# Post-norm decoder layer on one core: the low-rank product in plain fp32, the first two norms' scaling on ScalarE, and one more stage between gate and expansion

## What is computed

```
x = layernorm(x + attention(x))            # 32 heads of 32, 8 kv heads, rope, causal softmax, wo
x = layernorm(x + conv3(x, ctx))           # 3 taps over features, each tap scaled by a cosine
                                           # similarity of neighbouring ctx columns
x = layernorm(x + 2 * ffn(x))              # ffn: low = x A^T  (8 experts x rank 16 = 128 columns)
                                           # logits = x Wr^T + br (8 columns)
                                           # out = (low * 8 softmax(logits)) B
```

## Time and profile before

| | before |
|---|---|
| median of 3 runs | 1571.94 us (1571.41 to 1572.42) |
| profiled execution | 1568.54 us |
| its span | 1566.8 us |
| mean granted TensorE clock | 0.981 |
| TensorE matmuls busy | 1402.8 us (90%) |
| VectorE busy | 1215.3 us (78%) |
| ScalarE busy | 859.7 us (55%) |
| GpSimd busy | 969.3 us (62%) |

### The profile page before, as it was taken

One profiled execution on the slowest core, in us unless ns is written; L12 is line 12 of the kernel. 1 busy time (PEld: TensorE's weight loads), 2 busy tenths in 40 slices (PEclk: granted clock), 3 DMA queues, 4 the chain that ended last, 5 costly groups with the idle time before them and its releaser, 6 DMA issues. The chain is left out here.

```text
span 1566.8 us, 32397 instructions
## 1 busy us (share of the span) xinstructions
PE 1402.8 (90%) x8288; PEld 1051.4 (67%) x8288; DVE 1215.3 (78%) x4094; ACT 859.7 (55%) x3196; POOL 969.3 (62%) x873
## 2 busy tenths in 40 slices
PE   6899898999999898999985899999999999999985
PEld 4566666666666666666662677777777777777774
DVE  5777677776777677776776588888888888888886
ACT  5777777777777777777775233333333333333332
POOL 3766666666666666666664566656666666666652
PEclk9999999999999999999997999999999999999996
DMA  6343434444443434344456765565555655556541
GB/s 223 106 135 108 131 113 132 113 132 121 123 134 108 132 112 132 115 135 120 121 171 181 188 147 148 156 156 134 145 141 147 161 139 143 145 141 155 147 108 41
DMA packets 109005, 213.03 MB, mean 136 GB/s; under 512 B 26656, under 2 KB 32288, under 8 KB 108960
## 3 DMA queue, kind: packets, MB, share of 16 engines
q1 hardware_dynamic: 108960, 212.51, 49.0%
HBM read 131.83 MB, written 34.47 MB: 106 GB/s over the span
## 5 line engine op out<-in xcount | busy, mean ns | idle before, releaser
L439 PE MATMUL wo_ps<-weights,halves 128*128 128x512 f32 x2304 | 572.2, 400 | 12.1 <-DVE weights L617 12.1
L701 ACT ACTIVATE pexp<-sm,smin 128x128 f32<-128x128 f32 x1024 | 398.5, 391 | 209.0 <-DVE smin L568 168.8
L439 PEld LDWEIGHTS wo_ps<-weights,halves 128*128 128x128 f32 x2304 | 422.7, 189 | 128.9 <-issue 34.6
L1050 PE MATMUL wo_ps<-weights,halves 128*128 128x512 f32 x1488 | 398.6, 401 | 2.0 <-DVE yz L1152 2.0
L1421 POOL TENSOR_TENSOR prods<-prod,prods 128x512 fp32r<-128x512 f32 x192 | 267.0, 1392 | 197.7 <-ACT prods L1333 196.7
L821 POOL TENSOR_TENSOR pn<-pexp,prec 128x512 f32<-128x512 f32 x256 | 267.3, 1044 | 180.4 <-DVE prec L575 180.4
L1050 PEld LDWEIGHTS wo_ps<-weights,halves 128*128 128x128 f32 x1488 | 273.5, 190 | 60.0 <-issue 3.7
L1333 ACT CAST prods<-prod 128x512 fp32r<-128x512 f32 x192 | 118.7, 619 | 326.8 <-DVE prod L1192 318.7
L568 DVE CUSTOM_DVE_ANT_0 sm<-s_ps,mask_t 128x128 f32<-128x128 f32 x1024 | 237.4, 288 | 14.7 <-PE s_ps L469 5.1
L1061 PE MATMUL conv_ps<-prods,weights 128*128 128x512 f32 x576 | 174.7, 412 | 41.2 <-POOL prods L1421 39.8
L575 DVE RECIPROCAL prec<-psum_row 128x4 f32<-128x4 f32 x256 | 44.8, 175 | 201.3 <-ACT pexp L701 201.1
(11 more groups left out here) (103 smaller groups left out, 1732.7 us busy)
## 6 DMA issues: line engine op xcount, KB each, us to landing
att<-sim_scratch SPq DMA_DIRECT2D x192, 252.0 KB
pt<-blocks SPq DMA_DIRECT2D x640, 64.0 KB, 2.0
ctx_t<-in_ctx SPq DMA_DIRECT2D x32, 576.0 KB, 4.7
raw<-in_xT SPq DMA_DIRECT2D x32, 512.0 KB, 3.6
raw<-ot_scratch SPq DMA_DIRECT2D x32, 512.0 KB, 6.5
xn<-in_x SPq DMA_DIRECT2D x32, 512.0 KB, 7.2
out<-late SPq DMA_DIRECT2D x32, 512.0 KB, 3.0
ot_scratch<-ot SPq DMA_DIRECT2D x63, 256.0 KB, 2.1
```

The source lines that it names most:

```text
L439: mm = pe.matmul(qkv_ps[(par + g) % 2][:], xs[:, par, xl, k], w_sb[:, wl, g, k], start=(k == 0 and n == 0), stop=(k == KT - 1 and n == 2))
L701: ins = nc.scalar.activation(pexp[:, c % 2, i * P:(i + 1) * P], sm[:, c % 2, i * P:(i + 1) * P], ACT.Exp, bias=smin[:, c % 2, i:i + 1], sc ...
L1050: mm = pe.matmul(wo_ps[n][:], os_t[:, par, ol, k], wo_sb[:, wl, k, n * BANK:(n + 1) * BANK], start=(k == 0 and m == 0), stop=(k == KT - 1 ...
```

## The change

In `part2`:

- `reduce_rank` multiplies the unsplit fp32 transpose `xt` by an unsplit fp32 `wa_t`: eight products of 136 columns instead of sixteen fp32r matmuls of 272. `low_x2` and the first two steps of `route` go, `gate_low` reads PSUM, and `wa_t` is loaded by one DMA (544 KB) at the start of part 2. The two pieces in part 1 that split `wa` go; `wx` stays.
- VectorE's `normalise` becomes `normalise1` and `normalise2` on ScalarE (activation with scale and shift). `average` makes the negated mean for all norms, `invert_root` the shift.
- `turn_low`, `high_lt` and `low_lt` of a sequence move from the end of its step f to the start of its step z, and slots and orders shift.

```
 # slots and TensorE
-    CONV_AT = (8, 10, 12, 14, 15, 17)
-    FIRST_CONV_AT = (11, 13, 15, 17, 18, 20)
+    CONV_AT = (9, 11, 13, 15, 17, 20)
+    FIRST_CONV_AT = (11, 13, 15, 17, 19, 20)
         def reduce_rank(t):
-            wait(pe, xt_lo, after(t, 2, 2))
+            wait(pe, xt_in, after(t, 2, 2))
             for k in range(KT):
-                for xl in range(2):
-                    mm = pe.matmul(ffn_place(t)[0][:, 0:2 * LOWW], xt[:, xl, k],
-                                   wa_sb[:, k].rearrange("p l n -> p (l n)"),
-                                   start=(k == 0 and xl == 0), stop=(k == KT - 1 and xl == 1))
+                mm = pe.matmul(ffn_place(t)[0][:, 0:LOWW], xt[:, k], wa_t[:, k * LOWW:(k + 1) * LOWW],
+                               start=(k == 0), stop=(k == KT - 1))
         # step
-                if valid(z) and s == 2:
-                    expand(z)
+                if valid(z):
+                    if s == 1:
+                        turn_low(z)
+                    if s == 3:
+                        expand(z)
                 if valid(f):
-                    if s in (9, 10):
-                        turn_x2(f, par, s - 9)
-                    if s == 13:
+                    if s in (11, 12):
+                        turn_x2(f, par, s - 11)
+                    if s == 14:
                         reduce_rank(f)
-                    if s == 15:
-                        turn_low(f)
 # SyncE
+        sp.dma_start(wa_t[:], wa).then_inc(consts_in, 16)
 # VectorE
             elif n == 1:
                 wait(dve, conv_done, after(t, UNITS, TAPS * (half + 1)))
+                wait(dve, normed[1], after(t - 1, 1, 1))
-            if n == 2:
-                dve.tensor_scalar(nmean3[:], mv[n][:, 0:1], -1.0, None, ALU.mult)
+            dve.tensor_scalar(nmean[n][:], mv[n][:, 0:1], -1.0, None, ALU.mult)
-        def normalise(t, par, n):
-            ...
-            dve.tensor_scalar(dst, src, mv[n][:, 0:1], rstd[n][:], ALU.subtract, ALU.mult).then_inc(normed[n], 1)
-        def low_x2(t, n):
-            ...
-            dve.tensor_tensor(dst[:, 1], ffn_place(t)[n][:], dst[:, 0].bitcast(F32), ALU.subtract).then_inc(xt_lo, 1)
-            dve.tensor_copy(lowhi[:], ffn_place(t)[0][:, LOWW:2 * LOWW]).then_inc(low_step, 1)
-            dve.tensor_tensor(low[:], ffn_place(t)[0][:, 0:LOWW], lowhi[:], ALU.add).then_inc(low_step, 1)
-            dve.tensor_tensor(logit[:], low[:, HR:LOWW], br_t[:], ALU.add).then_inc(low_step, 1)
+            dve.tensor_tensor(logit[:], ffn_place(t)[0][:, HR:LOWW], br_t[:], ALU.add).then_inc(low_step, 1)
         # order of a step now: add(c,0,1) count(c,0,1) average(c,0) | low_lt(z) add(z,2,0) add(z,2,1) |
         # multiply(c,0) | add(f,1,1) count(f,1,1) average(f,1) | multiply(c,1) | count(z,2,0)
         # count(z,2,1) average(z,2) | multiply(c,2) | add(t,0,0) count(t,0,0) | multiply(c,3)
         # multiply(c,4) add(c,1,0) count(c,1,0) | route(f) | multiply(c,5) | gate_low(f)
 # ScalarE
+        def normalise1(t, par):
+            wait(act, shifted[0], after(t, 1, 1))
+            nc.scalar.activation(x1[:, par, 1:D + 1], yz[:, 0], ACT.Identity, bias=shift[0][:],
+                                 scale=rstd[0][:]).then_inc(normed[0], 1)
+        def normalise2(t, par):
+            wait(act, shifted[1], after(t, 1, 1))
+            nc.scalar.activation(x2[:, par], yz[:, 1], ACT.Identity, bias=shift[1][:],
+                                 scale=rstd[1][:]).then_inc(normed[1], 1)
         # order of a step now: high_o(t+1) high_lt(z) normalise1(c) high_prod(c,0) high_prod(c,1)
         # normalise2(f) high_prod(c,2) normalise3(z) copy_x2(f,0) high_prod(c,3) copy_x2(f,1)
         # high_prod(c,4) gates(f) high_prod(c,5)
 # GpSimd
             pool.tensor_tensor(rstd[n][:], var[n][:], power[:], ALU.pow).then_inc(rstd_done[n], 1)
-            if n == 2:
-                pool.wait_ge(rstd_done[n], after(t, 1, 1))
-                pool.tensor_tensor(shift3[:], nmean3[:], rstd[n][:], ALU.mult).then_inc(shifted, 1)
+            pool.wait_ge(rstd_done[n], after(t, 1, 1))
+            pool.tensor_tensor(shift[n][:], nmean[n][:], rstd[n][:], ALU.mult).then_inc(shifted[n], 1)
         # order of a step now: invert_root(c,0) low_o(t+1,0) low_prod(c,0) invert_root(f,1)
         # low_prod(c,1) invert_root(z,2) low_prod(c,2) low_o(t+1,1) low_prod(c,3..5)
```

More of the change, by code:

```diff
@@ L100, in later_weights @@
 def later_weights(weights):
-    hi, lo = (weights[:, part * NG * KT * BANK:(part + 1) * NG * KT * BANK] for part in range(2))
+    lo = weights[:, NG * KT * BANK:2 * NG * KT * BANK]
     both = weights[:].rearrange("p (l m) -> p l m", l=2)
@@ L916, in part2 @@
     late = sb("late", [P, 2, 2, D])
-    xt = sb("xt", [P, 2, KT, S], F32R)
+    xt = sb("xt", [P, KT, S])
+    wa_t = sb("wa_t", [P, KT * LOWW])
     br_t = sb("br_t", [P, H])
     id_t = sb("id2_t", [P, P])
-    lowhi = sb("lowhi", [P, LOWW])
-    low = sb("low", [P, LOWW])
     logit = sb("logit", [P, H])
@@ L933, in part2 @@
     rstd = [sb(f"rstd{n}", [P, 1]) for n in range(3)]
-    nmean3 = sb("nmean3", [P, 1])
-    shift3 = sb("shift3", [P, 1])
+    nmean = [sb(f"nmean{n}", [P, 1]) for n in range(3)]
+    shift = [sb(f"shift{n}", [P, 1]) for n in range(3)]
     x2, res = late[:, 0], late[:, 1]
@@ L966, in part2 @@
     held = sem("held2")
-    shifted = sem("shifted")
+    shifted = [sem(f"shifted{n}") for n in range(3)]
     stored = [sem("stored0"), sem("stored1")]
@@ L1120, in _ @@
         steps(pe, step, 0, B - 1, LEAD, TAIL - 3)
+        convolve(B - 2, 4)
+        turn_low(B - 3)
         convolve(B - 2, 5)
@@ L1292, in _ @@
         average(B - 1, 0)
+        low_lt(B - 3)
         add(B - 2, 0, 1, 1)
-        normalise(B - 1, 1, 0)
+        count(B - 2, 1, 1)
+        average(B - 2, 1)
         for m in range(PB):
             multiply(B - 1, 1, m)
-        count(B - 2, 1, 1)
-        average(B - 2, 1)
-        multiply(B - 1, 1, 3)
-        normalise(B - 2, 0, 1)
-        multiply(B - 1, 1, 4)
         finish(B - 3)
-        low_x2(B - 2, 0)
-        multiply(B - 1, 1, 5)
-        low_x2(B - 2, 1)
+        for m in range(PB, UNITS):
+            multiply(B - 1, 1, m)
         add(B - 1, 1, 1, 0)
@@ L1351, in normalise3 @@
         def normalise3(t, par):
-            wait(act, shifted, after(t, 1, 1))
+            wait(act, shifted[2], after(t, 1, 1))
             wait(act, stored[par], arrivals(t, par) - 16)
-            nc.scalar.activation(res[:, par], y3[:], ACT.Identity, bias=shift3[:], scale=rstd[2][:]).then_inc(normed[2], 1)
+            nc.scalar.activation(res[:, par], y3[:], ACT.Identity, bias=shift[2][:], scale=rstd[2][:]).then_inc(normed[2], 1)
         def step(t, par):
@@ L1361, in step @@
                 high_o(t + 1, 1 - par)
+            if valid(z):
+                high_lt(z)
             if valid(c):
+                normalise1(c, 1 - par)
                 high_prod(c, 0)
@@ L1382, in step @@
                 high_prod(c, 5)
-            if valid(f):
-                high_lt(f)
         steps(act, step, 0, B - 1, LEAD, TAIL - 3)
+        high_lt(B - 3)
+        normalise1(B - 1, 1)
+        normalise2(B - 2, 0)
         for m in range(UNITS):
             high_prod(B - 1, m)
-            if m in (3, 4):
-                high_x2(B - 2, m - 3)
+            if m in (2, 3):
+                copy_x2(B - 2, m - 2)
         normalise3(B - 3, 1)
+        normalise2(B - 1, 1)
         gates(B - 2)
-        high_x2(B - 1, 0)
+        copy_x2(B - 1, 0)
         high_lt(B - 2)
-        high_x2(B - 1, 1)
+        copy_x2(B - 1, 1)
         gates(B - 1)
@@ L1427, in step @@
             c, f, z = t - 1, t - 2, t - 3
+            early = not at_step(t, 0) and not at_step(t, 1)
             if valid(c):
                 invert_root(c, 0)
-            early = not at_step(t, 0) and not at_step(t, 1)
             if valid(t + 1) and early:
@@ L1438, in step @@
                 low_prod(c, 1)
-            if valid(t + 1) and early:
-                low_o(t + 1, 1 - par, 1)
+            if valid(z):
+                invert_root(z, 2)
             if valid(c):
@@ L1445, in step @@
                 low_o(2, 0, 1)
-            if valid(z):
-                invert_root(z, 2)
+            if valid(t + 1) and early:
+                low_o(t + 1, 1 - par, 1)
             if valid(c):
```

113 lines of the change are left out of this document (40 added, 73 removed).

## The result

| | before | after |
|---|---|---|
| median, on one chip | 1572.02 us | 1511.24 us (1509.29 to 1512.58) |
| ratio of medians | | 0.9613 (0.9596 to 0.9629) |
| profiled execution | 1568.54 us | 1512.58 us |
| its span | 1566.8 us | 1510.7 us |

Forecast were 1525 us and a range of 1513 to 1549.

The account below looks back on a forecast made before the run. TensorE was taken as nearly the bound, held up by waits for GpSimd's products; 48.1 us gained in periods plus 0.8, less 2.5 for the load, made 46.4, forecasting 1525.5 us, range 1513 to 1549.

Parts of the forecast that it names:

- the period: Steady steps of part 2: from 21.31 to 19.65 us, 48.1 us gained over 29 periods.
- the drain: After the last step: between 2 us gained and 3 lost, taken as nothing.
- the start of part 2: First steps of part 2: 2.5 us lost to the wa_t load, 0.8 gained as half a step's worth.
- the step from one execution to the median: Whole kernel: median put 3.4 us above the profiled execution, 1522.1 to 1525.5 us.
- the bound: Steps of part 2: TensorE's own work, 19.6 us per sequence, becomes the bound alone as 1.7 us of waiting goes.
- the order laid out by hand: One step of part 2: each engine's times set against TensorE's; all its waits go, thin margins 0.2, 0.5, 0.8 us.
- rival A: Steps of part 2: thin margins fail because VectorE and GpSimd still take turns; period 20.35, 1545.8 us; chance 0.21.
- D: Step boundary in part 2: a ring of waits sets the old 21.31 us period again, 1572 us; chance 0.04.
- B: Low rank on TensorE: plain fp32 costs four passes, 4.0 us, slower at 1589.5 us; chance 0.06.
- C: Low rank on TensorE: faster passes make it 1.5 us, 16 us less, 1509 us; chance 0.03.
- the low rank: TensorE in each step: eight plain fp32 products, two passes each at 0.125 us, 2.0 us, no change.
- 0.05 added for restarts: Steady period of part 2: 0.05 us added for TensorE restarts at the thin margins, giving 19.65 us.

Follow-up runs that it names:

- e1: Changed kernel with the low-rank product computed twice into the same bank; 1566.16 us, ratio 0.9976.
- e10: Changed kernel with each plain fp32 low-rank product on 272 columns instead of 136; 1565.30 us, ratio 0.9957.
- e7: Kernel before with only the plain fp32 low rank (no low_x2, wa_t loaded at the start of part 2); 1562.41 us, ratio 0.9954.
- e3: Changed kernel with the low rank split again into fp32r matmuls, low_x2 back on VectorE; 1534.87 us, ratio 0.9785.
- e11: The changed kernel itself, run again on one chip beside e12 and e13; 1510.06 us, ratio 0.9614.
- e12: Changed kernel with the wa_t load put behind the first loads of part 2, run beside e11; 1511.07 us, ratio 0.9612.
- e4: Changed kernel with norms 1 and 2 scaled by VectorE again, without the two shifts; 1532.29 us, ratio 0.9771.
- e13: As e12, and VectorE scales the three norms left after the last step; 1507.93 us, ratio 0.9599.
- e2: Same kernel as e12 in another session: changed kernel with wa_t loaded after the first loads of part 2; 1508.78 us, ratio 0.9618.
- e5: Changed kernel with turn_low, high_lt and low_lt back at the end of step f; 1521.33 us, ratio 0.9695.
- e14: Kernel before with GpSimd's second low_o moved behind low_prod 2; 1563.31 us, ratio 0.9948.
- e8: Kernel before with only normalise1 and normalise2 moved to ScalarE; 1558.48 us, ratio 0.9926.
- e6: Changed kernel with e3's and e4's edits together, leaving only slots, orders and the longer pipeline; 1575.38 us, ratio 1.0036.
- e9: Changed kernel with the low-rank product on 72 of its 136 columns; 1509.36 us, ratio 0.9597.

## Why the prediction was right in kind and wrong in size

Forecast and measured time differ by 14.3 us, and no single step of the forecast carries that: 5.0 us are the period, 3.6 the drain, 3.1 the start of part 2 (1.4 gained where 1.7 were to be lost), 4.6 the step from one execution to the median; 2.0 went the other way, ahead of part 2. What would bound the steady step and which waits would go was forecast right.

**Right: the bound.** The steady step is TensorE's own work. The 19.6 us read from the last full step became 19.48, and e1 shows that each us added to TensorE is a us of time.

**Right: the order laid out by hand.** Against the trace of the step that begins at 1176.58 or 1196.06: `low_lt` ended at 2.4 (forecast 2.6), the first multiply came at 5.1 (5.1), product 0 was ready at 7.9 (7.8), `normalise2` ended at 10.5 (10.6), product 1 at 10.6 (10.5), product 2 at 13.2 (13.3), the transposes' copies at 14.9 (15.1), the gate at 19.0 (19.4). All of these are within 0.4 us, so rival A (a wait comes back) fell. Some of it is luck. x1 was ready at 4.4, not 4.9, and did not set the first multiply: VectorE was adding norm 3 until then. And the turns between VectorE and GpSimd that A was built on did stay; they cost these two engines time, but TensorE no wait. D (a ring) fell with e1. B fell by its price, not by its rule. A product is two records of two clocks a column (e10), so four clocks a column, where fp32r takes one: the work of four passes. But a clock for each of 136 columns is 0.057 us, and 32 of those are 1.8 us; B, and the forecast too, put 0.125 on a pass, which is what 272 columns cost. The forecast's two passes came out near the truth because each record takes two clocks a column. The time lies nearer to C's 1509 than to the forecast, but C's mechanism, a low rank of 1.5 us, is not what happened either.

**Wrong in size: the low rank.** I took 2.0 us because sixteen fp32r matmuls take that the earlier trace rows and called it no change, though the earlier trace rows gave 0.11 to 0.12 a pass. It is 1.85: the fp32r matmul of 272 columns costs 0.125 where its columns at 2.4 GHz, one clock each, make 0.113, and the plain fp32 record of 136 columns, two clocks each, costs 0.116. This is 0.15 us in each of 29 periods, 4.4 us. With 0.05 added for restarts that didn't come, and 0.03 more TensorE work elsewhere than I read, the period is 0.17 shorter than the forecast: 5.0 us.

**Wrong: the drain, 0 forecast, 3.6 measured.** The plain fp32 low rank is on the path there, twice, ahead of the gate. Before, two subtractions and two sums of VectorE stood around it, and they are gone. e7, which has only this edit, has a drain of 40.1 us from the last projection against 45.5, but at a mean granted clock of 0.82 against 0.73. The cleaner pair is e3 and the changed kernel, which differ in the low rank alone and have the same mean clock, 0.83: 43.9 us against 41.9. So about 2 us are the low rank (e11 and e12, with the same drain, differ by 1.3). The two ScalarE scalings work against it: with VectorE in their place the drain is 1.5 to 2.8 us shorter (e4, e13). I had seen both signs and let them cancel. The clock differs too. The drain of the kernel before and of the changed one, columns as in the earlier trace rows:

```profile
1521.30:1566.80 45.50, 24.70 (x90) 18.08 (x89) 29.67 (x63) 10.66 (x19) 13.35 (x16) 0.73 0.16 51
```
```profile
1468.80:1510.70 41.90, 22.54 (x94) 16.16 (x92) 23.07 (x55) 14.11 (x23) 13.99 (x19) 0.83 0.18 57
```

The mean granted clock is 0.73 and 0.83 of 2.4 GHz, a mixture of the two levels, and TensorE idles less in the second. The last low-rank product took 2.85 us before, at a mean clock of 0.66, and 2.1 after, at 0.88; at the full clock the two cost 2.01 and 1.85. How much of the 3.6 us is the clock stays open.

**Wrong: the start.** I charged 2.5 us for the load of `wa_t`, taking its transfer as time added one to one. It is about half of that: 1.3 us later came the first product after the start of part 2, and the runs above give 1.1 to 1.3 on average. And the rest of the first steps, priced at half a step's gain, 0.8, gained 2.7 us. That the first matmul of part 2 came 2.0 us later is scatter: in runs whose first parts are alike (after, e1, e2, e4, e11, e12) it begins between 856.1 and 860.0.

**The bridge to the median.** I carried the 3.4 us between the profiled execution before and its median over to the kernel after, where the profiled execution lies on the other side of its median by 1.3. That is 4.6 us of the miss, and chance, not mechanism. The range reached 12.5 us below the forecast and had no room for it, the low rank, the start and the drain together.

**What the forecast's reasoning didn't say.** I explained the wait before by one collision. e14 removed it, and 0.34 us of the expected 1.1 a period came back. The three parts of the change don't add up either: alone they gain 0.15 (e7), 0.52 (e8) and -0.07 us (e6) of a loop period of 21.54; together 2.06. Each relief alone leaves or exposes another wait: e7 the old one, e14 the gate, e8 the scaling on ScalarE that the old slots ask for too early. The new order costs a little without the two reliefs (e6). With only one of them it gains 1.25 or 1.26 us (e3, e4), with both 2.06. That VectorE instructions with two inputs in SBUF and GpSimd's keep each other out is also what the Trainium skill says (SBUF — State Buffer, section "SBUF: two separate sides"): the pair of ports is an exclusive lock. The traces agree (1.69 us for a multiply of 0.68). But the rule prices one collision; it doesn't say where the next one falls, and e14's first case, worked out from one collision, was wrong.

## What to carry to other kernels

When one engine is to be the bound, read its work from a step in which it doesn't wait, and lay the new order out against it with the slack of each wait: that gave the steady period within 1%. Don't price a wait by the one collision seen in front of it: on engines that are nearly full, taking it away moves the time to the next wait, and reliefs that are worth little alone can be worth more than three times their sum together. Collisions need not go for a change to pay: here VectorE lost about 2 us a step to them before and after, but after the change none reached TensorE. Keep the terms outside the steady loop (start, drain, the offset between a profiled execution and the median) in the range: here they were as large as its margin. And take the cost of a group of matmuls from what it adds to the period, or from its start to a point one group further on: from its start to the next start alone it came out 0.09 us short here.

## What the runs showed of the hardware

- A plain fp32 product is two matmul records with a load each. At 272 columns they are 0.229 us apart, two clocks of 2.4 GHz for each column, at 136 0.116, at 72 still 0.112: below 136 next to nothing was left to save here.
- The fp32r low rank with its 272 columns cost 2.01 us for sixteen, the plain fp32 one with 136 columns 1.85, though both are 16 records of 272 clocks of columns: for 136 output columns the split saved nothing on TensorE and cost VectorE two subtractions, 1.4 us a step.
- At the full clock the weight loads of the plain fp32 product lasted 187 to 190 ns, those of the fp32r one 186 to 188: 2 ns between them. e9's, ahead of 72 columns, lasted up to 192.
- A VectorE sum of 8 columns with both inputs in SBUF took 1.30 us beside a GpSimd operation of 1.29 us, and 0.17 without it (e14).
